# Four variance sums of an attention stage regrouped and moved in TensorE's order

## The reference, cut to what matters

```python
y = jnp.moveaxis(ys, 0, 1) + x * D[None, None, :, None]
yg = y.reshape(B, L, G, GROUP_SIZE)
var = jnp.mean(yg * yg, axis=-1, keepdims=True)
yn = (yg * lax.rsqrt(var + EPS)).reshape(B, L, I) * norm_weight
yn = yn * jax.nn.silu(gate)
out = jnp.einsum('bli,di->bld', yn, out_proj_w)
x = x + out
```

## Time and profile before

| What | Value |
|---|---|
| median of 3 runs | 1615.36 us (1615.16 to 1615.81) |
| the profiled execution | 1614.37 us |
| its span | 1612.4 us, 32430 instructions |
| TensorE busy in matmuls | 1587.4 us, 98% |
| TensorE busy in weight loads | 1275.0 us, 79% |
| VectorE, ScalarE, GpSimd busy | 65%, 52%, 49% |
| granted clock, mean | 0.997 |

### The profile page before, as it was taken

The page is one execution under the profiler, slowest core; times in us unless marked ns, Lnnn a source line. Parts: engine busy times, 40 slices in busy tenths (PEclk is TensorE's granted clock), DMA queues, the critical chain, the costliest instruction groups (busy, mean ns, idle before and its releaser), DMA issues.

```text
span 1612.4 us, 32430 instructions
## 1 busy us (share of the span) xinstructions
PE 1587.4 (98%) x13001; PEld 1275.0 (79%) x13001; DVE 1049.8 (65%) x1707; ACT 845.7 (52%) x1372; POOL 787.5 (49%) x747
## 2 busy tenths in 40 slices
PE   8999999999999999999999999999999999999998
PEld 6778888888888888877777888888888888888666
DVE  6876666565656667576776656565766656565545
ACT  4654546555555555555455555555555655554321
POOL 3564645546363644544345454536454554633306
PEclk9999999999999999999999999999999999999999
DMA  5111102011111102011012111112020111113892
GB/s 191 59 54 33 41 21 66 28 53 40 40 53 34 51 12 64 27 53 40 22 50 77 53 40 40 54 34 59 10 64 21 53 40 47 47 36 85 200 210 107
DMA packets 50293, 93.19 MB, mean 58 GB/s; under 512 B 5664, under 2 KB 6304, under 8 KB 50144
## 3 DMA queue, kind: packets, MB, share of 16 engines
q1 hardware_dynamic: 50144, 91.11, 19.6%
HBM read 82.64 MB, written 8.45 MB: 56 GB/s over the span
## 4 chain that ended last, share of the span: by engine, by line
PE 86%; ACT 6%; DVE 3%; issue 3%; POOL 2%; POOLq 0%; DVEq 0%; ACTq 0%
PE PS L438 49%; PE PS L547 20%; PE PS L513 4%; PE PS L481 3%; PE PS L639 2%; ACT L798 2%; PE PS L597 2%; ACT big L791 1%; PE PS L528 1%; ACT Lt L798 1%; DVE cb L1023 1%; PE PS L391 1%; PE PS L493 1%; ACT oh L717 1%; PE PS L388 1%
## 5 line engine op out<-in xcount | busy, mean ns | idle before, releaser
L438 PE MATMUL PS<-xh,wh 128*128 128x512 f32 x1280 | 520.0, 406 | 0.6 <-DVE xl L955 0.6
L438 PE MATMUL PS<-xh,wl 128*128 128x512 f32 x1280 | 500.3, 391 | 0.0
L438 PE MATMUL PS<-xl,wh 128*128 128x512 f32 x1280 | 500.2, 391 | 0.0
L1023 DVE SCALAR_TENSOR_TENSOR cb<-PS,P,cb 128x496 f32<-128x496 f32 (+2 forms) x576 | 412.4, 716 | 130.6 <-ACT cb L759 117.0
L1318 POOL TENSOR_TENSOR wl<-rw,wh 128x512 fp32r<-128x512 f32 x160 | 212.6, 1334 | 187.4 <-ACT wh L710 172.3
L1338 POOL TENSOR_TENSOR ysum<-yq 128x256 f32<-128x256 f32 x128 | 109.4, 855 | 361.7 <-ACT yq L806 361.7
L438 PEld LDWEIGHTS PS<-xh,wl 128*128 128x128 f32 x1280 | 240.5, 188 | 53.1
L438 PEld LDWEIGHTS PS<-xh,wh 128*128 128x128 f32 x1280 | 240.8, 188 | 51.4 <-issue 1.0
L438 PEld LDWEIGHTS PS<-xl,wh 128*128 128x128 f32 x1280 | 241.2, 188 | 44.6
L759 ACT ACTIVATE cb<-PS,P 128x512 f32<-128x512 f32 x192 | 148.5, 774 | 205.1 <-PE PS L438 205.1
L1053 DVE TENSOR_TENSOR big<-Lt,gmt 128x512 f32<-128x512 f32 x128 | 102.3, 841 | 153.4 <-ACT Lt L798 153.4
(11 more groups left out here) (204 smaller groups left out, 2177.6 us busy)
## 6 DMA issues: line engine op xcount, KB each, us to landing
rw<-in_w_in SPq DMA_DIRECT2D x160, 256.0 KB, 2.7
ro<-in_w_out SPq DMA_DIRECT2D x64, 256.0 KB, 2.8
x2s<-acc SPq DMA_DIRECT2D x16, 260.0 KB, 5.4
out_x<-acc SPq DMA_DIRECT2D x16, 256.0 KB, 2.6
acc<-in_x SPq DMA_DIRECT2D x3, 1024.0 KB, 9.4
wh<-x2s SPq DMA_DIRECT2D x8, 260.0 KB, 5.0
wl<-x2s SPq DMA_DIRECT2D x8, 260.0 KB, 5.7
wh<-x2s SPq DMA_DIRECT2D x8, 259.5 KB, 5.6
```

What stands on the lines that cost most here:

```text
L438: mm = e.matmul(PS[:, proj_bank(n, m), :], w[:, m, 128 * k:128 * k + 128], v[:, k, a:a + 512], start=(i == 0), stop=(i == 11))
L1023: e.scalar_tensor_tensor(out=cv[:, :, d:32], in0=pv[:, :, 0:32 - d], scalar=P[:, P_CW + 4 * c + 3 - d:P_CW + 4 * c + 4 - d], in1=cv[:, :, ...
```

## The change

TensorE's orders of the stage before are changed: `S((0,))` goes from the end of slot 1 to slot 2, ahead of `Y(2)`, and the sums of tiles 1, 2 and 3 become one group at the end of slot 5. `variance` and `rstd` follow this grouping. VectorE's three `add_out` of tiles 1, 2 and 3 go to slot 6, and `add_out(0)` goes from ahead of `taps(2)` to behind them.

```diff
 def sums(n):
-    return ((0,), (1, 2), (3,)) if n < END else ((0, 1), (2, 3))
+    return ((0,), (1, 2, 3)) if n < END else ((0, 1), (2, 3))
...
-                elif group == (1, 2):
+                elif group == (1, 2, 3):
                     pe.wait_ge(G_masked, n + 1)
...
                     if m == 2:
                         if n:
+                            S(n - 1, (0,))
                             Y(n - 1, 2)
                             Y(n - 1, 3)
...
                         O(n - 1, i)
-                        if i != 1:
-                            S(n - 1, {0: (0,), 2: (1, 2), 3: (3,)}[i])
+                        if i == 3:
+                            S(n - 1, (1, 2, 3))
...
-                        if m in (2, 5, 6):
-                            variance(n - 1, {2: (0,), 5: (1, 2), 6: (3,)}[m])
+                        if m in (2, 6):
+                            variance(n - 1, {2: (0,), 6: (1, 2, 3)}[m])
...
-                        if m == 2:
-                            add_out(n - 1, 0)
-                        if m == 5:
+                        if m == 6:
                             add_out(n - 1, 1)
                             add_out(n - 1, 2)
-                        if m == 6:
                             add_out(n - 1, 3)
...
                     if m < 6:
                         taps(n, m)
+                    if n and m == 2:
+                        add_out(n - 1, 0)
...
-                        if m in (2, 5, 6):
-                            rstd(n - 1, {2: (0,), 5: (1, 2), 6: (3,)}[m])
+                        if m in (2, 6):
+                            rstd(n - 1, {2: (0,), 6: (1, 2, 3)}[m])
```

## The result

The changed kernel takes 1624.45 us (median of 4 runs, 1621.19 to 1624.58), the kernel before beside it on the same chip 1615.26 (4 runs, 1614.98 to 1615.81). The ratio is 1.0058 with a 95% interval of [1.0045, 1.0072]: slower by 0.6%. The forecast was 1620.4 with a range up to 1622.3. The sign and the places were right, the size was not: 9.2 us instead of 5.0.

What follows compares the result with a forecast made beforehand. The prediction took TensorE's issue order plus its waits as the bound. Terms 2.1 + 1.3 + 1.0 + 0.6 - 0.1 = +4.9, unrounded +5.0, on 1615.4 gave 1620.4 us, range 1616.5 to 1622.3.

Steps and rivals of the forecast that it cites:

- Stage 1: 2.46 - 1.32 + 0.2 = +1.3 us: `dt_turn` 2.46 us later behind `add_out(1)`, less `decay_sums`' vanished wait, plus slot 9's ordinary wait: +1.3 us.
- its like for stage 17: Same rows as stage 1, but with a `decay_sums` wait 0.3 us longer: +1.0 us.
- the hold by GpSimd: Stage 1, VectorE: GpSimd's 1.30 us operation holds the series' fourth step, ending the series at 104.41 instead of 103.49.
- Slot 9's new wait: Stage 1: once `decay_sums`' wait vanishes, slot 9 gets the ordinary wait for the exponential, 0.2 us.
- rival E: Even stages: late output-weight load holds ScalarE past slot 8, slot 9's wait grows; 1623.2 us, chance 0.08.
- Ordinary stages: The 27 repeating stages: +0.08 us each, +2.1 us in all.
- The 0.77 us for the group of three: Sums of tiles 1 to 3: 0.77 us together against 0.76 now, so grouping costs +0.01 us.
- `O(1)`'s wait: Slot 3: waiting for `add_out(0)` behind `taps(2)` loses the 0.13 us saved and 0.06 to 0.07 more.
- The bound of 0.73: Lower bound in us for the group of three, if only 0.22 us between the sums' starts were added.
- The first sum in slot 2: Ahead of `Y(2)` the sum costs 0.11 us against 0.25 in slot 1, gaining 0.13 to 0.14 a stage.
- stage 16: `variance` stands behind `mixed_lo`, so `add_out(1)` ends at 798.83 and `dt_turn` loads later: +0.6 us (0.3 to 1.0).
- stage 15: `mix_tile` stands behind slot 3's `proj`, so `O(1)` doesn't wait there: a gain of 0.12 us.

Runs made afterwards that it cites:

- the fillers: The changed kernel with ten useless 512-column matmuls ahead of `dt_turn` in stages 1 and 17: 1616.56 us against 1614.23, ratio 1.0017.
- the run in which the clock stayed up: The changed kernel with `split_o_lo(0)` of even stages put ahead of the three `add_out` in slot 6: 1619.35 us against 1614.23, ratio 1.0032.
- the two mended ones: The changed kernel with `split_o_lo(0)` first in slot 6 (1619.35 us); and that outside stages 1, 16, 17, which keep old order, plus `add_out(0)` ahead of `taps(2)` (1608.28 us).
- the repeat: The changed kernel once more, unaltered, on a third chip: 1620.1 us against 1614.31 for the kernel before, ratio 1.0037.

## Why the prediction was wrong

**The failed step** is "Stage 1: 2.46 - 1.32 + 0.2 = +1.3 us" and its like for stage 17. The wait was worked out nearly right: `add_out(1)` starts 1.20 instead of 1.04 behind `variance`, and the hold by GpSimd is 1.04 and not 0.92. What is missing is a term for TensorE's clock behind the idle time, 1.6 us in each of the two stages. It is shown by the fillers, which take the idle time away and keep the wait, and by the run in which the clock stayed up, whose two stages give +1.31 and +1.04. Slot 9's new wait costs 0.37 and 0.40 and not 0.2. So the two stages give 3.31 + 3.03 = 6.3 us out of the 2.3 forecast: 3.2 of the difference is the clock, 0.8 the rest. The step's 2.46 us of delay stood in my own text, but I never added up how long TensorE would then stand still.

The trace of the kernel before could have warned me. In stage 0 `G_all` waits 2.96 us for ScalarE, and the granted clock is 0.50 from 37.43 to 40.84 (first the row, then a window with the columns as above):

```profile
37.60 0.66 PE L493 MATMUL PS<-big 128*32 128x32 f32 x32 [2.96 <-ACT big L781]
```

```profile
37.50:40.50 3.00, 2.90 (x38) 2.36 (x39) 2.89 (x6) 1.71 (x4) 1.70 (x2) 0.50 0.00 0
```

**What makes up the 10.4 us** of the one trace, against 5.0, in round numbers: 3.2 the clock, 1.6 late loads, 1.1 stage 0, 0.8 the rest of stages 1 and 17, less 1.1 in the ordinary stages. The failed step is the largest part. Stage 0 and the late loads are not in every execution.

**Late loads, rival E.** I gave it 0.08 and let it go through the load behind `split_o_lo(0)`. That `split_o_lo(0)` ends 2.1 us later was right. The load behind it, the third of a stage, is issued as much later, and ScalarE waits for it, about 1.1 us in each even stage; TensorE doesn't feel that. The load that cost TensorE time in this trace is the next one, issued unchanged, now 1.2 us behind its neighbour and not 3.3. From issue to landing its median is 3.1 to 3.4 us in the seven traces with the three `add_out` in front of the split in every ordinary stage, and 2.5 to 2.6 in the five others, the two mended ones among them, where the two issues are 3.3 or 5.6 us apart. ScalarE's waits for both loads are 17.6 to 20.0 us in the seven and 1.9 to 2.3 in the five. So the order on VectorE makes both later. How much of it reaches TensorE varies: 1.6 us here, about nothing in the repeat; in three other traces the third load lands 3.6 us after its issue, in one or two stages, and costs 0.5 to 0.6 us each time.

**Ordinary stages.** The 0.77 us for the group of three was too high: it measures 0.69, against 0.76 for the old places. `O(1)`'s wait costs 0.25 and not 0.20. Together with the 0.06 or 0.07 saved this is 0.04 a stage, 1.0 us in all and not 2.1. The bound of 0.73 that I gave for the group was itself passed.

**The first sum in slot 2** (0.13 to 0.14 gained), **stage 16** (+0.6) and **stage 15** (-0.1) were right: 0.15, +0.58 and -0.19. The forecast of a line for L547's matmuls waiting on VectorE was wrong, for the reason given with the trace.

**Stage 0** added 1.06 us in the one trace and -1.13 in the repeat's. As one kernel gives both, it belongs to the execution. `G_all` of this stage waits 2.96 us for ScalarE in the trace before, 3.31 in the changed kernel's and 1.79 in the repeat's, and the stretch at half clock around its end lasts 3.4, 6.8 and 3.4 us. With the late loads stage 0 accounts for most of the difference between the two traces of this kernel, 10.4 and 6.3 us up to the last `proj`. Had the repeat been the measurement, 1620.1 would have met the forecast, but by luck, through errors that cancel. By its trace they are 3.2 us of clock drops and 0.8 more in stages 1 and 17 that I didn't count, against 1.1 us gained in stage 0 and 1.4 us that the ordinary stages didn't cost.

**Open** is why the clock fell behind `dt_turn`'s idle time of 3.05 to 3.23 us in both stages of four traces (two of them of the changed kernel, one of the grouping alone, one with `add_out(0)` ahead) and in neither stage of a fifth with 3.04 and 3.07; how often it falls in executions that weren't traced; and why a load takes up to 4.6 us to land in some stages only. Neither was tried further.

## What to carry to other kernels

When a change makes the busiest engine wait, write down how long it will stand still in one piece, and price what its clock does afterwards apart from the wait itself: one wait of 3 us cost half as much again. Look in the trace before for a stretch as long, and at the granted clock behind it. Before work is moved behind a long instruction on a side engine, list everything queued behind it, the operations that free a transfer's buffer too, since here the second of two loads issued close together landed later. Grouping and moving small products was worth 6 us here, once the block stages and `add_out(0)` had their old order back and `split_o_lo(0)` stood ahead of the three `add_out`.

## What the runs showed of the hardware

- In stages 1 and 17 the granted clock fell to 0.50 around TensorE's return from an idle stretch of 3.05 to 3.23 us, eight times in four traces: from 1.0 us ahead of the return to 1.3 us behind it. It stayed there 3.4 us, once 6.8. It didn't fall behind 0.78 and 0.93 us, nor in one trace behind 3.04 and 3.07. In stage 0 of the repeat it fell 0.7 us behind the end of a shorter one, of 1.79 us. The Trainium skill, "TensorE: Matmul & The Clock Gate", "Part 1: The HAM clock gate", says that the count behind the clock doesn't start with the kernel, so that the point of the switch varies; that would fit the exception, but no run here tests it.
- Sums of one column cost 0.25 us for one, 0.51 for two and 0.69 for three in a group, and 0.10 to 0.12 for one in front of the 64x64 products, which wait for their weight load anyway.
- The second of two 256 KB loads landed in a median of 3.1 to 3.4 us when it was issued 1.2 us behind the first, and in 2.5 to 2.6 when it was issued 3.3 or 5.6 us behind it.
- GpSimd's power takes 0.87 us on three columns.
